# Two factors' first columns as one stretch of a weight tile, its rows loaded in two halves by two queues

## The chip, the cores and the metric

The kernel runs on one core of a Trainium2 chip. The metric is the device time of one execution in microseconds (us); less is better. A kernel's time is the median of its runs.

## What is computed

For eight sequences of 128 tokens with 512 features, `x` goes through a linear layer with a low-rank adapter chosen for each sequence, then through a second linear layer with a routed low-rank part (the best two of 16 experts), and the input is added at the end. Cut to what matters:

```python
base_out = jnp.einsum('bti,oi->bto', x, W) + b               # L0_cond: W is 512 x 512
A, Bm = lora_As[adapter_mapping], lora_Bs[adapter_mapping]    # one adapter of 32 for a sequence
y = base_out + jnp.einsum('btr,bro->bto', jnp.einsum('bti,bir->btr', x, A), Bm) * 2.0

base_out = jnp.einsum('bsi,oi->bso', y, base_w) + base_b      # L0_ffn
res_hidden = jnp.einsum('bsi,ri->bsr', y, A)                  # R = 64
probs = jax.nn.softmax(jnp.einsum('bsi,ei->bse', y, router_w), axis=-1)
topw, topi = jax.lax.top_k(probs, 2)                          # of 16 experts, then normalised
delta = jnp.einsum('bse,bsr,eor->bso', combine, res_hidden, B)
out = x + base_out + delta * 0.5
```

## The kernel before

**The fold.** The two linear layers follow each other with nothing between them, so the kernel first multiplies their weights into one: W is one factor and the second layer's three matrices side by side (64 + 16 + 512 = 592 columns) are the other. On the way in, both stand beside each other in `w_cat`, in four chunks `k` of 128 rows: columns 0 to 511 are W, columns 512 to 1103 the second factor. The tile `w_raw` has the same layout in SBUF: 128 partitions, chunk `k`, 1104 columns. The product of chunk `k` is summed over `k` in four pairs of PSUM banks, `pairs[0]` to `pairs[3]`; pair `m` takes the 128 columns `m*128` to `m*128+127` of W as its stationary side.

**Split products.** To keep float32 accuracy every factor is split in a high and a low part (`w_hi`, `w_lo`), and every product is three matmuls: high by high, high by low, low by high. The high part is a cast (on ScalarE for W's columns, on VectorE for the second factor's), the low part a subtraction on VectorE.

**The start.** Chunk 0 is loaded in four pieces. ScalarE issues W's left half (`W_LEFT`, columns 0 to 255) and then its right half (`W_RIGHT`). SyncE issues the second factor's left half (`W2_LEFT`, 296 columns) and then its right half (`W2_RIGHT`). Each piece covers all 128 partitions and has a semaphore of its own. As pieces land, ScalarE casts W's left half in two steps of 128 columns and then the right half in one; VectorE casts `W2_LEFT`, subtracts for `W2_LEFT` and `W_LEFT`, casts `W2_RIGHT`, subtracts for `W2_RIGHT` and `W_RIGHT`. TensorE runs 13 matmuls on a tile of zeros (`WARM_UP`), and then the fold of chunk 0 in quarters: first the pairs of the first half of W's columns (m = 0, 1) against `W2_LEFT`, then against `W2_RIGHT`, then the other two pairs likewise. Each quarter has three groups of two matmuls, and each group waits for its operands: `wh_left`/`wh_done` count ScalarE's casts, `wh_first` VectorE's, `wl_first` and `wl_done` VectorE's subtractions. Chunks 1 to 3 follow whole, the one behind the other, on every engine.

**After the fold** the eight sequences go through as a pipeline: products of x with the folded weights, routing, expert products. Every engine's order is written out by hand; semaphores alone order the engines among each other.

All matmuls are issued by the helper `mm` at L820, so that the profile has one line for all of them.

Of the kernel before, what the change touches and what calls it, by code (L numbers as in the profile page):

```python
# [15 lines left out]
ACT = mybir.ActivationFunctionType  # L16
AX_X = mybir.AxisListType.X

P = 128
NT = 8  # L20
D = 512
KC = D // P
# [31 lines left out]
FOLDS = (1, 0, 2, 3)  # L54

W_LEFT, W_RIGHT = slice(0, D // 2), slice(D // 2, D)
W2_LEFT, W2_RIGHT = slice(D, D + W2H), slice(D + W2H, D + W2N)
WARM_UP = 13

ACT_TABLES = 2  # L60
# [2 lines left out]
def adaln_ffn_kernel(nc, x_t, x_n, w_cat, tables, slots, b1, b2, experts, out):  # L63
    with ExitStack() as ctx:
# [6 lines left out]
        def sem(name):  # L71
            return ctx.enter_context(nc.semaphore(name))
# [5 lines left out]
        w_raw = w_raw_all[:, :].rearrange("p (k n) -> p k n", k=KC)  # L78
# [10 lines left out]
        w_hi = w_hi_all[:, :].rearrange("p (k n) -> p k n", k=KC)  # L89
# [85 lines left out]


        in_w = [None] + [sem(f"in_w{k}") for k in range(1, KC)]
        in_w_side = [sem("in_w_left"), sem("in_w_right")]
        in_w2_side = [sem("in_w2_left"), sem("in_w2_right")]
        in_w_next = sem("in_w_next")  # L180
        in_slots = sem("in_slots")
        in_lora = sem("in_lora")
# [9 lines left out]
        stored = sem("stored")  # L192

        wh_first = sem("wh_first")
        wh_left = sem("wh_left")
        wh_next = sem("wh_next")
        wh_done = sem("wh_done")
        wl_first = sem("wl_first")
        wl_done = sem("wl_done")
# [59 lines left out]
        def _(sp):  # L259
# [1 line left out]
                sp.dma_start(w_raw[:, k, :], w_cat[k]).then_inc(in_w[k], 16)  # L261


            for n, cols in enumerate((W2_LEFT, W2_RIGHT)):
                sp.dma_start(w_raw[:, 0, cols], w_cat[0, :, cols]).then_inc(in_w2_side[n], 16)

            sp.dma_start(w_raw[:, 1, D // 2:], w_cat[1, :, D // 2:]).then_inc(in_w[1], 16)
            sp.dma_start(w_raw[:, 1, W_LEFT], w_cat[1, :, W_LEFT]).then_inc(in_w_next, 16)
# [86 lines left out]
            for half in range(2):  # L355
                cols = slice(half * D // 2, (half + 1) * D // 2)
# [56 lines left out]

        @block.scalar
        def _(act):
            for n, cols in enumerate((W_LEFT, W_RIGHT)):
                act.dma_start(w_raw[:, 0, cols], w_cat[0, :, cols]).then_inc(in_w_side[n], 16)
            act.wait_ge(in_w_side[0], 16)
            for cols in (slice(0, P), slice(P, 2 * P)):
                nc.scalar.activation(w_hi[:, 0, cols], w_raw[:, 0, cols], ACT.Copy).then_inc(wh_left, 1)  # L420
            act.wait_ge(in_w_side[1], 16)
            nc.scalar.activation(w_hi[:, 0, W_RIGHT], w_raw[:, 0, W_RIGHT], ACT.Copy).then_inc(wh_done, 1)
            act.wait_ge(in_slots, 16)
            for t in range(NT - ACT_TABLES, NT):
                slot = act.value_load(slot_row[0:1, t:t + 1], min_val=0, max_val=SLOTS - 1)
# [160 lines left out]
        def _(dve):  # L586
# [10 lines left out]
            nc.vector.memset(low_row[F_BIAS:F_BIAS + 1, :], 0.0).then_inc(first_set, 1)  # L597

            def first_block_hi(n, cols):
                dve.wait_ge(in_w2_side[n], 16)  # L600
                nc.vector.tensor_copy(w_hi[:, 0, cols], w_raw[:, 0, cols]).then_inc(wh_first, 1)

            def first_block_lo(cols, done):
                nc.vector.tensor_tensor(w_lo[:, 0, cols], w_raw[:, 0, cols], w_hi[:, 0, cols].bitcast(F32),
                                        ALU.subtract).then_inc(done, 1)

            first_block_hi(0, W2_LEFT)
            dve.wait_ge(wh_first, 1)
            first_block_lo(W2_LEFT, wl_first)
            dve.wait_ge(wh_left, 2)  # L610
            first_block_lo(W_LEFT, wl_done)
            first_block_hi(1, W2_RIGHT)
            dve.wait_ge(wh_first, 2)
            first_block_lo(W2_RIGHT, wl_first)
            dve.wait_ge(wh_done, 1)
            first_block_lo(W_RIGHT, wl_done)
            for k in range(1, KC):
                dve.wait_ge(in_w[k], 16)
                nc.vector.tensor_copy(w_hi[:, k, D:], w_raw[:, k, D:]).then_inc(wh_first, 1)
# [190 lines left out]
            for half in range(2):  # L810
                cols = slice(half * D // 2, (half + 1) * D // 2)
# [6 lines left out]
        def _(pe):  # L818
            def mm(out_ap, lhs, rhs, first, last):
                return nc.tensor.matmul(out_ap, lhs, rhs, start=first, stop=last)  # L820
# [5 lines left out]

            for _ in range(WARM_UP):
                mm(ps_warm, idle[:, 0:P], idle, True, True)
# [6 lines left out]
            def fold_quarter(m, lhs, rhs, out_cols, cols, first):  # L835
                mm(pairs[m][:, out_cols], lhs[:, 0, m * P:(m + 1) * P], rhs[:, 0, cols], first, False)

            sides = ((slice(BANK - W2H, BANK), W2_LEFT), (slice(BANK, BANK + W2H), W2_RIGHT))
            for half, rows_done in enumerate((wh_left, wh_done)):
                ms = range(half * KC // 2, (half + 1) * KC // 2)  # L840
                for side, (out_cols, cols) in enumerate(sides):
                    pe.wait_ge(wh_first, side + 1)
                    for m in ms:
                        pe.wait_ge(rows_done, 1 if half else m + 1)
                        fold_quarter(m, w_hi, w_hi, out_cols, cols, True)
                    pe.wait_ge(wl_first, side + 1)
                    for m in ms:
                        fold_quarter(m, w_hi, w_lo, out_cols, cols, False)
                    pe.wait_ge(wl_done, half + 1)
                    for m in ms:  # L850
                        fold_quarter(m, w_lo, w_hi, out_cols, cols, False)
# [240 lines left out]
```

## Time and profile before

| | us |
|---|---|
| median of three runs | 101.38 |
| lowest, highest | 101.21, 102.25 |
| the profiled execution, its whole time | 101.33 |
| the span of its instructions | 99.5 |
| TensorE busy in the span | 95.6 |
| VectorE, ScalarE, GpSimd busy | 66.6, 41.5, 22.2 |

The whole time of the profiled execution is 1.83 us more than its span: what lies around the instructions. The trace is of that one execution. Its times are in us from the start of the span; engines are PE (TensorE matmuls), PEld (its weight loads), DVE (VectorE), ACT (ScalarE), POOL (GpSimd) and SP (SyncE); a q behind a name is the engine's sequencer, which issues the DMAs.

### The profile page before, as it was taken

The page shows a single profiled execution, that of the slowest core. Times are in us where ns is not written, and L with a number is a line of the kernel's source. Part 1 is how long each engine was busy: PE and PEld are TensorE (multiplying, and loading weights), DVE is VectorE, ACT ScalarE, POOL GpSimd, SP SyncE. Part 2 cuts the span into 40 slices and gives each one's busy share as a digit, 9 for nine tenths or more (in the row PEclk, how much of TensorE's full clock was granted, in tenths as well). Part 3 has the DMA queues.
Part 4 walks back from the last instruction along what each step waited for, and adds up shares of the span by engine and source line. Part 5 has one row for each costly group of instructions (what it writes and reads, how often), then busy time and mean ns, then how long its engine had stood idle before and what let it go on. Part 6 is the DMA issues. An engine that isn't in the chain of part 4 may idle for free.

```text
span 99.5 us, 1810 instructions
## 1 busy us (share of the span) xinstructions
PE 95.6 (96%) x572; PEld 87.0 (87%) x572; DVE 66.6 (67%) x184; ACT 41.5 (42%) x101; POOL 22.2 (22%) x34
## 2 busy tenths in 40 slices
PE   6799999999999999999999999999999999999990
PEld 6699999999999999998898799888787877878980
DVE  5669996997485885899977567257949275572101
ACT  3514636968787546756522610451334022040000
POOL 4100004224999965108123000000000000000000
PEclk9999999999999999999999999999999999999999
DMA  1999659999558675891780836516228074020211
GB/s 42 331 326 410 207 123 361 267 361 352 150 91 205 203 239 151 232 231 37 221 253 25 214 119 163 153 43 184 106 76 255 26 194 122 0 105 0 105 59 53
DMA packets 8379, 16.91 MB, mean 170 GB/s; under 512 B 1507, under 2 KB 4067, under 8 KB 8370
## 3 DMA queue, kind: packets, MB, share of 16 engines
q1 hardware_dynamic: 7762, 16.41, 55.1%
q10 hardware_dynamic: 576, 0.39, 1.2%
q8 instruction: 5, 0.08, 0.3%
q14 instruction: 4, 0.03, 0.1%
q0 software_dynamic: 32, 0.00, 0.0%
HBM read 13.28 MB, written 2.16 MB: 155 GB/s over the span
## 4 chain that ended last, share of the span: by engine, by line
PE 93%; DMA 3%; DVE 0%; ACT 0%; issue 0%
PE pair L820 90%; DMA w_raw_all<-w_cat 3%; PE pair L965 1%; PE pair L967 1%; PE pair L985 1%; DVE xn L814 0%; ACT w_hi_all L420 0%; PE pair L955 0%; PE pair L944 0%; PE pair L942 0%; PE pair L934 0%
## 5 line engine op out<-in xcount | busy, mean ns | idle before, releaser
L820 PE MATMUL pair<-e_hi,w_hi_all 128*128 128x512 f32 (+1 forms) x72 | 27.1, 376 | 0.0
L820 PE MATMUL pair<-e_hi,w_lo_all 128*128 128x512 f32 (+1 forms) x72 | 26.7, 370 | 0.0
L820 PE MATMUL pair<-e_lo,w_hi_all 128*128 128x512 f32 (+1 forms) x72 | 26.7, 370 | 0.0
L533 ACT ACTIVATE w_hi_all<-exp_raw_all 128x512 fp32r<-128x512 f32 x16 | 9.7, 630 | 15.3 <-DVE exp_raw_all L755 15.3
L820 PEld LDWEIGHTS pair<-e_hi,w_lo_all 128*128 128x128 f32 x72 | 13.6, 188 | 2.5
L820 PEld LDWEIGHTS pair<-e_hi,w_hi_all 128*128 128x128 f32 x72 | 13.6, 188 | 2.5
L820 PEld LDWEIGHTS pair<-e_lo,w_hi_all 128*128 128x128 f32 x72 | 13.6, 189 | 2.0
L762 DVE TENSOR_TENSOR w_lo_all<-exp_raw_all,w_hi_all 128x512 fp32r<-128x512 f32 x16 | 10.4, 689 | 4.5 <-ACT w_hi_all L533 4.0
L755 DVE TENSOR_TENSOR exp_raw_all<-w_raw_all 128x512 f32<-128x512 f32 x16 | 11.2, 741 | 0.1
L769 DVE TENSOR_TENSOR xn<-pair,xn 128x512 f32<-128x512 f32 x7 | 4.8, 690 | 8.9 <-PE pair L820 8.9
L820 PE MATMUL pair<-p_hi,x_hi 128*128 128x304 f32 x32 | 10.0, 311 | 0.0
L820 PE MATMUL pair<-p_hi,w_hi_all 128*128 128x304 f32 x32 | 9.9, 308 | 0.0
L820 PE MATMUL pair<-p_lo,x_hi 128*128 128x304 f32 x32 | 9.7, 303 | 0.0
L820 PE MATMUL pair<-p_lo,w_hi_all 128*128 128x304 f32 x32 | 9.7, 302 | 0.0
L820 PE MATMUL pair<-p_hi,w_lo_all 128*128 128x304 f32 x32 | 9.7, 302 | 0.0
L820 PE MATMUL pair<-p_hi,x_lo 128*128 128x304 f32 x32 | 9.7, 302 | 0.0
L376 POOL TENSOR_TENSOR w_lo_all<-xt_raw,w_hi_all 128x512 fp32r<-128x512 f32 x4 | 5.2, 1293 | 13.7 <-ACT w_hi_all L438 10.6
L394 POOL TENSOR_TENSOR e_lo<-exp_raw_all,e_hi 128x1024 fp32r<-128x1024 f32 x3 | 7.2, 2399 | 0.0
L820 PE MATMUL pair<-w_hi_all 128*128 128x296 f32 x32 | 6.1, 301 | 0.5 <-ACT w_hi_all L420 0.5
L820 PEld LDWEIGHTS pair<-p_hi,w_hi_all 128*128 128x128 f32 x32 | 6.0, 188 | 0.3
L820 PEld LDWEIGHTS pair<-p_lo,w_hi_all 128*128 128x128 f32 x32 | 6.0, 189 | 0.2
L820 PE MATMUL pair<-w_lo_all,w_hi_all 128*128 128x296 f32 x32 | 6.1, 302 | 0.0
(107 smaller groups left out, 162.2 us busy)
## 6 DMA issues: line engine op xcount, KB each, us to landing
w_raw_all<-spill SPq DMA_DIRECT2D x16, 256.0 KB, 4.2
xt_raw<-x_t SPq DMA_DIRECT2D x4, 512.0 KB, 6.3
exp_raw_all<-experts SPq DMA_DIRECT2D x4, 512.0 KB, 8.7
xn<-x_n SPq DMA_DIRECT2D x4, 512.0 KB, 5.8
out<-xn SPq DMA_DIRECT2D x7, 256.0 KB, 2.8
w_raw_all<-w_cat SPq DMA_DIRECT2D x2, 552.0 KB, 6.4
c_stack<-c_hi SPq DMA_DIRECT2D x7, 74.0 KB, 3.9
c_stack<-c_lo SPq DMA_DIRECT2D x7, 74.0 KB, 4.2
```

What stands on the lines that cost most here:

```text
L376: pool.tensor_tensor(x_los[t % XB], xt_raw[:, t, :].rearrange("p (k n) -> p k n", k=KC), x_his[t % XB].bitcast(F32), ALU.subtract).then_in ...
L394: pool.tensor_tensor(e_lo[:, js, :], exp_raw[:, js, :], e_hi[:, js, :].bitcast(F32), ALU.subtract).then_inc(el_pool_done, 1)
L533: nc.scalar.activation(gt_hi[:, t % 2, js, :], g[:, js, :], ACT.Copy).then_inc(gh_done, 1)
L755: nc.vector.tensor_tensor(g[:, js, :], weight_rows[:, b, js, :], hidden[:, b, :].unsqueeze(1).to_broadcast([P, GH, P]), ALU.mult).then_inc ...
L762: nc.vector.tensor_tensor(gt_lo[:, t % 2, js, :], g[:, js, :], gt_hi[:, t % 2, js, :].bitcast(F32), ALU.subtract).then_inc(gl_done, 1)
L769: nc.vector.tensor_tensor(xn[:, t, :], ps_d[t % 2], xn[:, t, :], ALU.add).then_inc(out_done, 1)
L820: return nc.tensor.matmul(out_ap, lhs, rhs, start=first, stop=last)
L965: nc.tensor.matmul(ps_z[par][:, z_small[par]:BANK], ht[:, par, :], c_stack[0:HT, t, 0:border], start=False, stop=True, skip_group_check=True)
L967: nc.tensor.matmul(ps_z[par][:, BANK:BANK + W2N - border], ht[:, par, :], c_stack[0:HT, t, border:], start=False, stop=True, skip_group_ch ...
L985: nc.tensor.transpose(ps_rt[0:cols, :], routed[:, t % 2, 0:cols], ident[:, :]).then_inc(pe_rt, 1)
```

## The change

Chunk 0 is cut into pieces in another way. W's right half and the second factor's left half are neighbours in `w_cat` and in `w_raw`; together they are one stretch of 552 columns, `LEAD` (columns 256 to 807). This stretch is now the first piece. SyncE loads its rows 0 to 63, ScalarE its rows 64 to 127, and both transfers count on one semaphore, `in_lead`. Behind its half SyncE loads `W2_RIGHT` as before, and ScalarE loads W's left half, which is now `W_REST`. The fold of chunk 0 begins with the pairs 2 and 3 (W's right half) and goes on to 0 and 1. Both ScalarE's first cast and VectorE's first cast wait for `in_lead` to reach 32, that is for both halves of the rows. The names `wh_left` and `in_w_side`, `in_w2_side` go.

```diff
+W_LEAD, W_REST = W_RIGHT, W_LEFT
 W2_LEFT, W2_RIGHT = slice(D, D + W2H), slice(D + W2H, D + W2N)
+LEAD = slice(W_LEAD.start, W2_LEFT.stop)
...
-            for n, cols in enumerate((W2_LEFT, W2_RIGHT)):
-                sp.dma_start(w_raw[:, 0, cols], w_cat[0, :, cols]).then_inc(in_w2_side[n], 16)
+            sp.dma_start(w_raw[0:P // 2, 0, LEAD], w_cat[0, 0:P // 2, LEAD]).then_inc(in_lead, 16)
+            sp.dma_start(w_raw[:, 0, W2_RIGHT], w_cat[0, :, W2_RIGHT]).then_inc(in_w2_right, 16)
...
-            for n, cols in enumerate((W_LEFT, W_RIGHT)):
-                act.dma_start(w_raw[:, 0, cols], w_cat[0, :, cols]).then_inc(in_w_side[n], 16)
-            act.wait_ge(in_w_side[0], 16)
-            for cols in (slice(0, P), slice(P, 2 * P)):
-                nc.scalar.activation(w_hi[:, 0, cols], w_raw[:, 0, cols], ACT.Copy).then_inc(wh_left, 1)
-            act.wait_ge(in_w_side[1], 16)
-            nc.scalar.activation(w_hi[:, 0, W_RIGHT], w_raw[:, 0, W_RIGHT], ACT.Copy).then_inc(wh_done, 1)
+
+            act.dma_start(w_raw[P // 2:, 0, LEAD], w_cat[0, P // 2:, LEAD]).then_inc(in_lead, 16)
+            act.dma_start(w_raw[:, 0, W_REST], w_cat[0, :, W_REST]).then_inc(in_rest, 16)
+            act.wait_ge(in_lead, 32)
+            for cols in (slice(2 * P, 3 * P), slice(3 * P, 4 * P)):
+                nc.scalar.activation(w_hi[:, 0, cols], w_raw[:, 0, cols], ACT.Copy).then_inc(wh_lead, 1)
+            act.wait_ge(in_rest, 16)
+            nc.scalar.activation(w_hi[:, 0, W_REST], w_raw[:, 0, W_REST], ACT.Copy).then_inc(wh_done, 1)
...
             def first_block_hi(n, cols):
-                dve.wait_ge(in_w2_side[n], 16)
+                if n == 0:
+                    dve.wait_ge(in_lead, 32)
+                else:
+                    dve.wait_ge(in_w2_right, 16)
...
-            for half, rows_done in enumerate((wh_left, wh_done)):
-                ms = range(half * KC // 2, (half + 1) * KC // 2)
+            for half, rows_done in enumerate((wh_lead, wh_done)):
+
+                ms = range((1 - half) * KC // 2, (2 - half) * KC // 2)
```

ScalarE's queue at the start of the program, before: two transfers of all 128 rows, then the table load and the casts of W's columns, each half behind its own semaphore.

```order
L417 DMA w_raw_all<-w_cat 128x256 x2
L420 ACT_TABLE_LOAD
L420 ACTIVATE w_hi_all<-w_raw_all 128x128 [waits in_w_left]
L420 ACTIVATE w_hi_all<-w_raw_all 128x128
L422 ACTIVATE w_hi_all<-w_raw_all 128x256 [waits in_w_right]
```

ScalarE's queue at the same place, now:

```order
L421 DMA w_raw_all<-w_cat 64x552
L422 DMA w_raw_all<-w_cat 128x256
L425 ACT_TABLE_LOAD
L425 ACTIVATE w_hi_all<-w_raw_all 128x128 [waits in_lead]
L425 ACTIVATE w_hi_all<-w_raw_all 128x128
L427 ACTIVATE w_hi_all<-w_raw_all 128x256 [waits in_rest]
```

The casts stand where they stood; the first transfer has half the rows and a little over twice the columns, and the first cast waits for the semaphore on which SyncE's half counts too.

VectorE's queue for chunk 0, before:

```order
L601 CAST w_hi_all<-w_raw_all 128x296 [waits in_w2_left]
L604 TENSOR_TENSOR w_lo_all<-w_raw_all,w_hi_all 128x296 [waits wh_first]
L604 TENSOR_TENSOR w_lo_all<-w_raw_all,w_hi_all 128x256 [waits wh_left]
L601 CAST w_hi_all<-w_raw_all 128x296 [waits in_w2_right]
L604 TENSOR_TENSOR w_lo_all<-w_raw_all,w_hi_all 128x296 [waits wh_first]
L604 TENSOR_TENSOR w_lo_all<-w_raw_all,w_hi_all 128x256 [waits wh_done]
```

VectorE's queue for chunk 0, now:

```order
L609 CAST w_hi_all<-w_raw_all 128x296 [waits in_lead]
L612 TENSOR_TENSOR w_lo_all<-w_raw_all,w_hi_all 128x296 [waits wh_first]
L612 TENSOR_TENSOR w_lo_all<-w_raw_all,w_hi_all 128x256 [waits wh_lead]
L609 CAST w_hi_all<-w_raw_all 128x296 [waits in_w2_right]
L612 TENSOR_TENSOR w_lo_all<-w_raw_all,w_hi_all 128x296 [waits wh_first]
L612 TENSOR_TENSOR w_lo_all<-w_raw_all,w_hi_all 128x256 [waits wh_done]
```

The six steps keep their order and their sizes; the first of them no longer waits for SyncE's piece alone.

## Rows read from the trace of the kernel before

**Rows 1.** The page, part 1: busy us, share of the span, instructions of each engine.

```profile
PE 95.6 (96%) x572; PEld 87.0 (87%) x572; DVE 66.6 (67%) x184; ACT 41.5 (42%) x101; POOL 22.2 (22%) x34
```

**Rows 2.** The chain that ended last, in order of time: start us, us, what.

```profile
0.74 3.15 DMA w_raw_all<-w_cat
...
3.92 0.32 ACT w_hi_all L420
...
4.37 20.75 PE pair L820 x148
...
96.98 0.42 DVE xn L814
```

**Rows 3.** SyncE's two transfers of chunk 0 (L265): issue ns, starts, landing.

```profile
L265 SPq DMA_DIRECT2D w_raw_all<-w_cat x2: 401/406/412, 0.7 to 1.2; - x2
...
DMA to landing us min/median/max: 3.0/3.1/3.2
```

**Rows 4.** ScalarE's two transfers of chunk 0 (L417): the same columns.

```profile
L417 ACTq DMA_DIRECT2D w_raw_all<-w_cat x2: 413/436/458, 0.7 to 1.2; - x2
...
DMA to landing us min/median/max: 3.2/3.2/3.3
```

**Rows 5.** VectorE's timeline from 3.6 us: start, us, instruction [idle before <-releaser].

```profile
3.73 0.32 DVE L601 CAST w_hi_all<-w_raw_all 128x296 fp32r<-128x296 f32 x1 [0.58 <-DMA w_raw_all<-w_cat]
4.08 0.80 DVE L604 TENSOR_TENSOR w_lo_all<-w_raw_all,w_hi_all 128x296 fp32r<-128x296 f32 x2
4.80 0.31 DVE L601 CAST w_hi_all<-w_raw_all 128x296 fp32r<-128x296 f32 x1
5.14 0.81 DVE L604 TENSOR_TENSOR w_lo_all<-w_raw_all,w_hi_all 128x296 fp32r<-128x296 f32 x2
6.64 0.47 DVE L619 CAST w_hi_all<-w_raw_all 128x592 fp32r<-128x592 f32 x1 [0.69 <-DMA w_raw_all<-w_cat]
```

**Rows 6.** ScalarE's timeline from 3.6 us, the same columns.

```profile
3.92 0.51 ACT L420 ACTIVATE w_hi_all<-w_raw_all 128x128 fp32r<-128x128 f32 x2 [0.96 <-DMA w_raw_all<-w_cat]
4.55 0.42 ACT L422 ACTIVATE w_hi_all<-w_raw_all 128x256 fp32r<-128x256 f32 x1
```

**Rows 7.** TensorE's timeline to 8 us, matmuls (PE) and weight loads (PEld).

```profile
0.78 3.04 PE L820 MATMUL pair<-const-float32-0.0 128*128 128x256 f32 x13 [0.78 <-PEq L1085]
...
4.37 0.51 PE L820 MATMUL pair<-w_hi_all 128*128 128x296 f32 x2 [0.55 <-ACT w_hi_all L420]
...
4.72 0.43 PE L820 MATMUL pair<-w_lo_all,w_hi_all 128*128 128x296 f32 x2
...
5.32 0.43 PE L820 MATMUL pair<-w_hi_all 128*128 128x296 f32 x2
...
5.66 0.30 PEld L820 LDWEIGHTS pair<-w_lo_all,w_hi_all 128*128 128x128 f32 x2 [0.16 <-DVE w_lo_all L604]
5.67 0.54 PE L820 MATMUL pair<-w_lo_all,w_hi_all 128*128 128x296 f32 x2
...
6.32 0.44 PE L820 MATMUL pair<-w_hi_all 128*128 128x296 f32 x2
...
7.95 1.26 PE L820 MATMUL pair<-w_hi_all 128*128 128x296 f32 x8
```

**Rows 8.** Five stretches: us, busy time of each engine, granted clock, DMA share, GB/s.

```profile
2.50:3.40 0.90, 0.90 (x6) 0.90 (x6) 0.40 (x5) 0.46 (x1) 0.35 (x3) 1.00 1.08 377
22.20:23.50 1.30, 1.30 (x12) 1.30 (x11) 1.23 (x2) 1.14 (x3) 0.00 (x0) 1.00 1.04 410
60.60:63.30 2.70, 2.70 (x19) 2.48 (x18) 1.97 (x4) 0.00 (x0) 0.00 (x0) 1.00 0.97 245
80.00:82.70 2.70, 2.70 (x13) 2.17 (x12) 2.50 (x4) 1.24 (x2) 0.00 (x0) 1.00 0.94 227
96.98:99.40 2.42, 0.00 (x0) 0.00 (x0) 0.42 (x1) 0.00 (x0) 0.00 (x0) 0.96 0.16 54
```

**Rows 9.** DMA issues from 59.3 to 63.3 us: times, KB each, us to landing.

```profile
w_raw_all<-spill SPq DMA_DIRECT2D x2, 256.0 KB, 3.9
```

More of the change, by code:

```diff
@@ L177, in adaln_ffn_kernel @@
         in_w = [None] + [sem(f"in_w{k}") for k in range(1, KC)]
-        in_w_side = [sem("in_w_left"), sem("in_w_right")]
-        in_w2_side = [sem("in_w2_left"), sem("in_w2_right")]
+        in_lead = sem("in_lead")
+        in_rest = sem("in_rest")
+        in_w2_right = sem("in_w2_right")
         in_w_next = sem("in_w_next")
@@ L194, in adaln_ffn_kernel @@
         wh_first = sem("wh_first")
-        wh_left = sem("wh_left")
+        wh_lead = sem("wh_lead")
         wh_next = sem("wh_next")
@@ L609, in _ @@
             first_block_lo(W2_LEFT, wl_first)
-            dve.wait_ge(wh_left, 2)
-            first_block_lo(W_LEFT, wl_done)
+            dve.wait_ge(wh_lead, 2)
+            first_block_lo(W_LEAD, wl_done)
             first_block_hi(1, W2_RIGHT)
@@ L615, in _ @@
             dve.wait_ge(wh_done, 1)
-            first_block_lo(W_RIGHT, wl_done)
+            first_block_lo(W_REST, wl_done)
             for k in range(1, KC):
@@ L838, in _ @@
             sides = ((slice(BANK - W2H, BANK), W2_LEFT), (slice(BANK, BANK + W2H), W2_RIGHT))
-            for half, rows_done in enumerate((wh_left, wh_done)):
-                ms = range(half * KC // 2, (half + 1) * KC // 2)
+            for half, rows_done in enumerate((wh_lead, wh_done)):
+                ms = range((1 - half) * KC // 2, (2 - half) * KC // 2)
                 for side, (out_cols, cols) in enumerate(sides):
                     pe.wait_ge(wh_first, side + 1)
-                    for m in ms:
-                        pe.wait_ge(rows_done, 1 if half else m + 1)
+                    for n, m in enumerate(ms):
+                        pe.wait_ge(rows_done, 1 if half else n + 1)
                         fold_quarter(m, w_hi, w_hi, out_cols, cols, True)
```

## The prediction

> **What bounds the kernel now.** I read the page first: TensorE is busy for 95.6 of 99.5 us [rows 1], no other engine for more than 67 percent. The chain of waits followed back from the end says the same: from 4.37 us on it is all TensorE, and ahead of that stand one transfer, one cast of ScalarE and nothing else [rows 2]. So a change to the loads of chunk 0 can act only through the moment from which TensorE runs without a break. The reader should now look for that moment, and it is not 4.37. The fold's first pair of matmuls starts at 4.37, released by ScalarE's cast. Undisturbed, a pair takes about 0.27 us from start to start: from the pair at 6.32 to the eight matmuls at 7.95 lie six pairs in 1.63 us. At the beginning pairs start at 4.37, 4.72, 5.32 and 5.67, and at 5.66 the weight load is idle for 0.16 us until VectorE's subtraction (L604) [rows 7]. TensorE is fed there by VectorE, whose row of work has no hole: it begins at 3.73 with the cast, goes on at 4.08, 4.80, 5.14 and is through at 5.95 [rows 5]. Behind 5.67 TensorE waits for nobody, and its operands are there early: chunk 1 is cast by VectorE at 6.64 to 7.11 [rows 5] and wanted at 7.95 [rows 7].
>
> The moment that decides is therefore the **start of VectorE's first cast**, 3.73 us, set by the landing of SyncE's first piece: issued at 0.75, landed 3.0 us later [rows 3]. ScalarE's first piece lands 0.2 us later, at 3.2 us behind an issue at 0.74 [rows 4], and ScalarE starts at 3.92 [rows 6]. That W's left half comes later costs the first pair of matmuls something, but not the end of the chunk, as long as VectorE is the one that is late at 5.67.
>
> **The change, part by part.**
>
> *The wait of VectorE (the term that counts).* VectorE's first cast used to wait for SyncE's 148 KB alone. It now waits for both halves of the lead piece, 138 KB on each queue. Queued behind it on VectorE are the five other steps of chunk 0; TensorE waits for each of them. The two first pieces hold 276 KB before and after, so the last byte of them should land when the last byte lands now, which is ScalarE's 3.9 us. If so, VectorE starts at 3.92 instead of 3.73: **+0.19 us**. All six steps move by that much, and with them the group of matmuls that waits for the subtraction at 5.67: it starts at 5.86. Nothing behind it can give that back, since TensorE is then busy to the end.
>
> *Size of the packets, a gain.* The rows of the lead piece are 2208 bytes long, where they were 1024 and 1184. The rate of the two first pieces in flight together is 377 GB/s (2.50 to 3.40 us); the best stretch of long rows over all partitions has 410 [rows 8]. 276 KB are 282.6 thousand bytes, 0.75 us at the one and 0.69 us at the other: at most 0.06 us earlier.
>
> *Half the partitions, a loss.* No transfer of the kernel before loads 64 rows from each of two queues. The nearest rows are the loads of routing weights from DRAM, each 256 KB for 64 partitions [rows 9]: in the stretches in which they fill the engines (share 0.97 and 0.94) these move 245 and 227 GB/s, not 377 to 410 [rows 8]. If the two halves ran at the slower of these, 282.6 thousand bytes would take 1.25 us, 0.50 us more than 0.75. But there one queue works through one half of the partitions and then the other, and each source row is read for 64 partitions. Here the halves are issued within 0.01 us of each other from two queues and run at the same time over all 128 partitions, as the two pieces do now. The nearest row for that is the present start, 377 GB/s. I take the loss of the halves and the gain of the longer rows as equal, together 0, and keep both ends: the landing moves by −0.06 to +0.50 us, VectorE's start by +0.13 to +0.69 us.
>
> The Trainium skill has a rule against this change, on its page "DMA: Bandwidth & Descriptors", section "Rules for kernel authors": of two transfers to disjoint halves of the partitions it says "Don't bother — they serialize", because both halves spread over the same 16 DMA engines. What the row shows is less than a queue for one: SyncE's and ScalarE's first pieces land 0.2 us apart though 128 KB alone need 0.35 us at 377 GB/s, so two pieces from two queues share the engines, they do not follow each other. Read to the letter, the rule would put the second half 0.37 us (138 KB at 377 GB/s) behind a first one that lands at 3.7, at 4.07, and the sum would be +0.34 instead of +0.19 us.
>
> *ScalarE and TensorE's first pair.* ScalarE starts its casts at 3.92 as before (3.86 at the best). VectorE's cast needs 0.32 us and ScalarE's first step about as long [rows 2, 5], so the operands of the first matmul are there at 4.24 and it starts at 4.37, as now: **0**. The next group needs the subtraction, which ends at 4.74 instead of 4.55 and so pushes the pair from 4.72 to about 4.87. These small gaps are the same 0.19 us, seen earlier; they are not added.
>
> *The other pieces.* `W2_RIGHT` lands 3.2 us behind an issue at 1.2, at 4.36 [rows 3]; VectorE now wants it at 4.80 + 0.19. ScalarE's second piece lands 3.3 us behind 1.2 and its cast runs from 4.55 to 4.97 [rows 4, 6]; TensorE wants it at 6.32. Both have 0.4 us or more to spare: **0**. The order of the pairs (2, 3 before 0, 1) changes no count and no size: **0**. The number of transfers is the same, and an issue of 0.4 us stays one of 0.4 us: **0**, and the queues behind are where they were. Chunk 1 lets VectorE idle for 0.69 us at 6.64 [rows 5], which takes up any delay of its own; TensorE's delay is not taken up.
>
> **The sum.** 101.33 (this execution) + 0.19 = 101.52 us. This execution lies 0.05 us under the median of the runs, so against the median it is 101.38 + 0.19 = **101.57 us**. That is 0.2 percent more. About 1 percent, 1.0 us, is what a measurement of this kernel can tell from no change.
>
> **Rivals.**
>
> *The halves are slow (loss up to 0.50 us).* For it speaks the rate of the loads for 64 partitions. The Trainium skill ("DMA: Bandwidth & Descriptors", section "The descriptor swizzle") says that in a transfer over 128 partitions each DMA engine writes one port of its own, and engines 0 to 7 write partitions 0 to 63; a half that spreads over all 16 would share ports. The trace shows no ports. Against it speaks that both halves run together. It gives +0.34 to +0.69 us, 101.7 to 102.1.
>
> *The piece lands earlier than SyncE's does now.* Longer rows might be worth more than the row of 410 GB/s shows, or SyncE's and ScalarE's halves might be closer to the present first landing at 3.7. Then ScalarE starts up to 0.2 us earlier, VectorE no later than now, and the first block ends where it ends today or up to 0.13 us earlier: 101.25 to 101.4. Against it: the whole 276 KB must be there, and 0.2 us of 377 GB/s are 75 KB that nobody takes off the engines.
>
> *VectorE's start isn't what decides.* If TensorE's group at 5.67 has slack that the trace hides, the start of the first matmul counts, and that doesn't move: 101.38, no effect. Against it is the hole of 0.16 us at 5.66.
>
> *Slower by over 1 percent: the clock.* The 13 warm-up matmuls of 256 columns take 3.04 us, 0.21 us from start to start, which is 1.2 GHz; the fold's 296 columns take 0.136 us, which is near 2.4 GHz [rows 7] (the clock row gives 1.00 for both, so the cadence has to tell). Between them TensorE is idle for 0.55 us. If late halves stretch this hole to 1 us and the clock then falls, as much work as the warm-up fills, 3.04 us at the low level, costs half of it too much: +1.5 us on top of the +0.69, 103.6. The point is whether the longer hole lets the clock fall. Against it: behind the last matmul, TensorE has nothing to do for 2.42 us and the mean granted clock of that stretch is still 0.96 [rows 8]; so most of 2 us of idleness leave it at the upper level. And with an unchanged first matmul the hole doesn't grow at all.
>
> **How the numbers follow.** Chances: 0.60 for the forecast (VectorE +0.13 to +0.33 us, 101.5 to 101.7); 0.20 for slow halves; 0.10 for an earlier landing; 0.06 for no effect; 0.02 for the clock; 0.02 for what I don't see. The range takes in the forecast, no effect, slow halves and the earlier landing, and some 0.1 us at the lower end for the spread of the runs (the lowest is 0.17 under the median): 101.15 to 102.1. Only the clock's case lies over 1 percent, and with a stray median I give it 0.04; no case reaches 1 percent faster, since the whole wait for the first piece would have to shrink by a third, and a stray median gets 0.02; within 1 percent 0.94.
>
> **What the profile of the changed kernel would show.** Right: VectorE's first cast and ScalarE's first cast start within 0.05 us of each other, near 3.9; the first fold matmul near 4.37; a wait for VectorE's subtraction of about 0.2 us or more ahead of the fifth group; that group near 5.86; TensorE without a break behind it; and the span 0.2 us longer. Slow halves: both casts at 4.1 to 4.4. Earlier landing: both at 3.75 or before. No effect: the casts late, but the eight matmuls of chunk 1 still at 7.95 and not at 8.14. The clock: fold matmuls 0.25 us apart behind the hole. I would be wrong above all if half-height transfers from two queues get in each other's way in a manner that no row of this trace shows.

## The result, and the profile after

The changed kernel is slower: **103.46 us** (102.46 to 104.62, six runs) against 101.35 (101.21 to 102.25). The ratio is **1.0135, with a 95% interval of 1.0085 to 1.0185**. The forecast was 101.57 with a range up to 102.1; the time lies outside it. The ratio and its interval, here and in all experiments, leave out runs over 1.5 percent above the fastest of the same kernel (here 104.62, which is the profiled one, and 104.52), so they are not the quotient of the medians.

The profiled execution of the changed kernel took 104.62 us, the longest of the six, and its span is 102.8. Not all of the 3.3 us that the span has over that of before is the change's. The chain of the kernel after, in order of time (start us, us, what):

```profile
0.76 3.48 DMA w_raw_all<-w_cat
...
4.26 0.32 DVE w_hi_all L609
...
4.71 22.31 PE pair L828 x148
27.03 0.11 PE pair L943
...
98.88 0.42 DVE xn L822
```

The last addition starts at 98.88 where it started at 96.98 [rows 2]: 1.90 us later. The other 1.4 us lie behind it, where only the last stores are left and nothing was changed. (An experiment below, the one with the joined wait, has the same: its last addition is at 96.95 and its span 100.9.) So the reader should use a mark inside the program. I take TensorE's **first transposition**, L943 here at 27.03, the first line after the 148 matmuls. The same piece in the chain of the kernel before:

```profile
25.13 0.11 PE pair L934
```

It too is 1.90 us later. The whole difference ahead of the last stores arises before the mark, and from there both kernels run alike up to the last addition. (1.90 us is the distance of two single executions; the one of the kernel before took 101.33 us, less than most of its runs beside the experiments.)

TensorE's timeline of the kernel after, to 10 us:

```profile
4.71 0.83 PE L828 MATMUL pair<-w_hi_all 128*128 128x296 f32 x2 [0.82 <-DVE w_hi_all L609]
5.34 0.69 PE L828 MATMUL pair<-w_lo_all,w_hi_all 128*128 128x296 f32 x2
5.84 0.69 PE L828 MATMUL pair<-w_hi_all,w_lo_all 128*128 128x296 f32 x2
...
8.30 0.63 PE L828 MATMUL pair<-w_lo_all,w_hi_all 128*128 128x296 f32 x2
8.77 0.44 PE L828 MATMUL pair<-w_hi_all,w_lo_all 128*128 128x296 f32 x2
9.04 0.44 PE L828 MATMUL pair<-w_hi_all 128*128 128x296 f32 x2
```

The first matmul is 0.34 us late, where the prediction had it unchanged at 4.37. And then pairs of matmuls (two matmuls that the trace shows as one row) start 0.49 us apart, 0.247 us for one of 296 columns: that is 1.2 GHz, the lower level of TensorE's clock. Only from 8.77 on are they 0.27 us apart, the cadence that the kernel before has in its fold [rows 7]. Up to its ninth pair the kernel before needs 2.50 us (4.37 to 6.87), this one 4.06: 1.56 us more. 0.34 + 1.56 is the 1.90 us. The 1.56 us are less than the clock alone costs: eight pairs at 0.272 us would be 2.18 us, so the low clock costs 1.88 us, and the 0.32 us that TensorE lost between its first pairs before [rows 7] no longer show. The matmuls have no idle stretch between them; the loss doesn't show in any list of waits, and the granted clock of the stretch reads 1.00. What tells is the distance from start to start. (The low clock isn't special to this long execution: experiments 6 and 10 have it in profiled executions of 103.60 and 103.17 us.)

ScalarE's timeline of the kernel after:

```profile
0.76 0.57 ACTq L421 DMA_DIRECT2D w_raw_all<-w_cat  x1
1.37 0.84 ACTq L422 DMA_DIRECT2D w_raw_all<-w_cat  x1
2.24 1.28 ACT L425 ACT_TABLE_LOAD   x1 [2.24 <-issue]
4.26 0.51 ACT L425 ACTIVATE w_hi_all<-w_raw_all 128x128 fp32r<-128x128 f32 x2 [0.74 <-DMA w_raw_all<-w_cat]
6.61 0.42 ACT L427 ACTIVATE w_hi_all<-w_raw_all 128x256 fp32r<-128x256 f32 x1 [1.84 <-DMA w_raw_all<-w_cat]
7.49 1.42 ACTq L432 DMA_DIRECT2D lora_raw<-tables  x2
8.96 0.72 ACT L435 ACTIVATE w_hi_all<-w_raw_all 128x256 fp32r<-128x256 f32 x2 [1.93 <-issue]
```

Two things here answer to [rows 4] and [rows 6]. The issues of the transfers take 0.57 and 0.84 us, where both took 0.41 to 0.46. And `W_REST` is cast at 6.61, not at 4.55: its transfer, issued at 1.37, needs 5.2 us to land, where the piece in its place needed 3.3. Behind it ScalarE's slot loads and adapter transfers are late, and with them its casts for chunk 1.

SyncE's half and ScalarE's half of the lead (L268 and L421), first the one, then the other:

```profile
L268 SPq DMA_DIRECT2D w_raw_all<-w_cat x1: 571/571/571, 0.7 to 0.7; - x1
...
DMA to landing us min/median/max: 2.9/2.9/2.9
```

```profile
L421 ACTq DMA_DIRECT2D w_raw_all<-w_cat x1: 570/570/570, 0.8 to 0.8; - x1
...
DMA to landing us min/median/max: 3.5/3.5/3.5
```

The halves are issued together and land 0.6 us apart, at 3.7 and 4.2.

### The profile page after: what moved, and what is told of

The parts are those of the page before. It is cut to its first block, busy times and chain, and to the rows that moved or that the text cites. A ratio compares the mean times of both kernels' runs of the same rounds, so it can differ in the third digit from the quotient of the medians.

```text
span 102.8 us, 1810 instructions
## 1 busy us (share of the span) xinstructions
PE 97.2 (95%) x572; PEld 88.8 (86%) x572; DVE 66.3 (64%) x184; ACT 41.4 (40%) x101; POOL 21.8 (21%) x34
## 4 chain that ended last, share of the span: by engine, by line
PE 92%; DMA 3%; DVE 1%; issue 0%
PE pair L828 88%; DMA w_raw_all<-w_cat 3%; PE pair L974 1%; PE pair L976 1%; PE pair L994 1%; DVE xn L822 0%; DVE w_hi_all L609 0%; PE pair L964 0%; PE pair L953 0%; PE pair L951 0%; PE pair L943 0%
## 5 line engine op out<-in xcount | busy, mean ns | idle before, releaser
L828 PE MATMUL pair<-w_hi_all 128*128 128x296 f32 x32 | 6.9, 331 | 0.8 <-DVE w_hi_all L609 0.8
L828 PE MATMUL pair<-w_lo_all,w_hi_all 128*128 128x296 f32 x32 | 6.7, 325 | 0.0
L828 PE MATMUL pair<-w_hi_all,w_lo_all 128*128 128x296 f32 x32 | 6.5, 317 | 0.0
L828 PEld LDWEIGHTS pair<-w_hi_all 128*128 128x128 f32 x32 | 5.6, 214 | 1.1 <-DVE w_hi_all L609 1.1
```

## The experiments

There are three suspects: the low clock, the late `W_REST`, and the transfers of 64 rows behind both. Theories A to D are those of each experiment's own expectation; a letter doesn't mean the same in all of them. Times are compared as ratios, since the kernel before measured 101.9 to 102.0 beside these runs. The hole is TensorE's idle time between its last warm-up matmul and the first one of the fold. The mark is the first transposition of one profiled execution each: 25.13 before, 27.03 after.

**1. More warm-up in the changed kernel.** TensorE's hole ahead of the fold is filled.

```diff
-WARM_UP = 13
+WARM_UP = 18
```

> The changed kernel with 18 warm-up matmuls instead of 13, which fills TensorE's idle stretch ahead of the fold (3.89 to 4.71 us in the profile after). Theory A (most of the 2 us come from the fold running at the low level of TensorE's clock, since the hole of 0.82 us keeps the clock from rising): the fold's matmuls are back at 0.136 us from start to start early on, and the time falls from 103.5 to about 102.0 (what is left is the later start and the late W_REST). Theory B (the loads alone cost it: lead piece at 4.24, W_REST at 6.59): no better than 103.3, or worse by the added warm-up.

103.29 us, ratio 1.0106 (1.0024 to 1.0187), mark at 27.11. Five of the six runs lie at 103.3 to 103.5 and one at 101.84. Theory A, which had 102.0, falls in this form. TensorE's timeline of this kernel:

```profile
4.69 0.51 PE L828 MATMUL pair<-w_hi_all 128*128 128x296 f32 x2 [0.20 <-DVE w_hi_all L609]
...
6.54 0.43 PE L828 MATMUL pair<-w_hi_all,w_lo_all 128*128 128x296 f32 x2
7.46 0.51 PE L828 MATMUL pair<-w_hi_all 128*128 128x296 f32 x2 [0.49 <-ACT w_hi_all L427]
7.80 0.44 PE L828 MATMUL pair<-w_lo_all,w_hi_all 128*128 128x296 f32 x2
...
9.86 0.92 PE L828 MATMUL pair<-w_hi_all 128*128 128x296 f32 x5 [0.53 <-ACT w_hi_all L435]
```

The clock is up from the first fold matmul, as theory A wanted, and nothing is won: TensorE now waits twice, at 7.46 for the cast of `W_REST` and at 9.86 for ScalarE's cast of chunk 1. In the changed kernel's own profile these waits were hidden, since TensorE at half speed came to both places when the data was there. From the first matmul of the fold to the first of chunk 1 the kernel before needs 3.58 us (4.37 to 7.95 [rows 7]), this one 5.17 (4.69 to 9.86) and the changed kernel 5.15 (4.71 to 9.86). So two costs of about 1.6 us cover for each other.

**2. The same in the kernel before.** `WARM_UP = 18` there.

> The kernel before with 18 warm-up matmuls instead of 13. At the low level the warm-up then ends at about 4.9 us, 0.5 us behind the present start of the fold. Theory A: the hole of 0.55 us goes, the spread of the kernel before (101.2 to 102.25) shrinks, the median lies between 101.2 and 101.8. Theory B: the fold starts up to 0.5 us later, 101.6 to 101.9, and the spread stays.

101.65 us, ratio 0.9999 (0.9957 to 1.0041), mark at 25.45. The longer warm-up is neither a gain nor a loss within what this can tell. In the one execution the fold starts at 4.60, 0.23 us later, and the mark is 0.32 us later; the spread stays (101.1 to 102.6), as theory B had it.

**3. Only the joined wait.** The kernel before, with VectorE's first cast behind both first pieces.

```diff
             def first_block_hi(n, cols):
+                if n == 0:
+                    dve.wait_ge(in_w_side[0], 16)
                 dve.wait_ge(in_w2_side[n], 16)
```

> The kernel before, with one more wait: VectorE's first cast also waits for ScalarE's first piece, as in the change; all transfers as before. By the prediction's sum +0.19 us (101.55). If joining the two waits is what matters beyond that, 102 or more; if the transfers in halves matter, it stays at 101.4 to 101.6.

102.28 us, ratio 1.0019 (0.9974 to 1.0063), mark at 25.10. In this execution ScalarE's piece landed early enough that both casts began at 3.71; the forecast's 0.19 us can't be told from zero here, and by the interval the joined wait alone costs 0.6 us at most.

**4. Only the order of the work.** The changed kernel with whole-height pieces and a semaphore for each.

```diff
-            sp.dma_start(w_raw[0:P // 2, 0, LEAD], w_cat[0, 0:P // 2, LEAD]).then_inc(in_lead, 16)
+            sp.dma_start(w_raw[:, 0, W2_LEFT], w_cat[0, :, W2_LEFT]).then_inc(in_w2_left, 16)
...
-            act.dma_start(w_raw[P // 2:, 0, LEAD], w_cat[0, P // 2:, LEAD]).then_inc(in_lead, 16)
+            act.dma_start(w_raw[:, 0, W_LEAD], w_cat[0, :, W_LEAD]).then_inc(in_lead, 16)
...
```

ScalarE's first cast waits for `in_lead` to reach 16, VectorE's for `in_w2_left`.

> The changed kernel's order of work (pairs 2 and 3 first, W's right half loaded first) with the transfers of the kernel before: each piece over all 128 partitions with a semaphore of its own. Theory A and B alike, both of which blame the transfers in halves: 101.3 to 101.6, as before. If the order of the pairs costs something: 102 or more.

102.06 us, ratio 1.0002 (0.9960 to 1.0044), mark at 25.13. The order of the pairs costs nothing that can be told, as forecast. With the joined wait out too, the lead piece in halves is what is left, as a long stretch or as half the height; the next two experiments separate these.

**5. The lead stretch in one piece.** SyncE loads all 128 rows of it, ScalarE only `W_REST`.

```diff
-            sp.dma_start(w_raw[0:P // 2, 0, LEAD], w_cat[0, 0:P // 2, LEAD]).then_inc(in_lead, 16)
+            sp.dma_start(w_raw[:, 0, LEAD], w_cat[0, :, LEAD]).then_inc(in_lead, 16)
...
-            act.dma_start(w_raw[P // 2:, 0, LEAD], w_cat[0, P // 2:, LEAD]).then_inc(in_lead, 16)
...
```

Both waits for `in_lead` go from 32 to 16.

> The changed kernel with the lead stretch in one transfer of all 128 rows, from SyncE; ScalarE issues W_REST alone. Theory A (transfers of 64 rows are slow to be issued and to begin: 0.57 us where 128 rows took 0.41, and the two halves run one behind the other): the lead's issue is back at about 0.41 us, it lands at 3.9 or before, W_REST lands by 4.6, the fold's last-but-early marker (the first transposition of TensorE) stands near 25.1 to 25.3 instead of 27.0 us, the time is as before. Theory B (the long rows of 2208 bytes are what is slow): the issue stays at 0.57 us or more, the lead lands at 4.2 or later.

102.09 us, ratio 1.0037 (1.0011 to 1.0064), mark at 25.21. The lead transfer of this kernel:

```profile
L268 SPq DMA_DIRECT2D w_raw_all<-w_cat x1: 402/402/402, 0.7 to 0.7; - x1
...
DMA to landing us min/median/max: 3.0/3.0/3.0
```

The same 552 columns, twice the rows and the bytes, and it is issued in 0.40 us and lands at 3.8, before the second half does in the changed kernel. The width is innocent. The loss isn't quite gone: the interval lies 0.1 to 0.6 percent above the kernel before.

**6. Halves at the narrow widths.** The kernel before, its two first pieces each as two halves of 64 rows.

```diff
+            sp.dma_start(w_raw[0:P // 2, 0, W2_LEFT], w_cat[0, 0:P // 2, W2_LEFT]).then_inc(in_w2_side[0], 16)
+            sp.dma_start(w_raw[0:P // 2, 0, W_LEFT], w_cat[0, 0:P // 2, W_LEFT]).then_inc(in_w_side[0], 16)
...
+            act.dma_start(w_raw[P // 2:, 0, W2_LEFT], w_cat[0, P // 2:, W2_LEFT]).then_inc(in_w2_side[0], 16)
+            act.dma_start(w_raw[P // 2:, 0, W_LEFT], w_cat[0, P // 2:, W_LEFT]).then_inc(in_w_side[0], 16)
...
```

`W2_RIGHT` and `W_RIGHT` follow whole; the first casts wait for both halves of their piece.

> The kernel before with its two first pieces each cut in halves of 64 rows over the two queues, at their narrow widths (296 and 256 columns); two transfers more in all. Theory A (half height is what costs): each half takes as long to issue as the wide halves did, about 0.57 us, so the first pieces land past 4.4 and W_RIGHT past 6.5, and the first transposition stands at 27 us or later. Theory B (width costs): issues of 0.41 us and less, first transposition by 25.6.

103.58 us, ratio 1.0158 (1.0107 to 1.0208), mark at 27.28. Its transfers by ScalarE, two of 64 rows and then one of 128:

```profile
0.76 0.57 ACTq L417 DMA_DIRECT2D w_raw_all<-w_cat  x1
1.35 0.86 ACTq L418 DMA_DIRECT2D w_raw_all<-w_cat  x1
2.25 0.60 ACTq L419 DMA_DIRECT2D w_raw_all<-w_cat  x1
2.89 1.28 ACT L422 ACT_TABLE_LOAD   x1 [2.89 <-issue]
```

0.57 us again at 296 columns: it is the height that makes the issue long. The transfer of 128 rows right behind the halves is slow too: `W_RIGHT` 0.60 us, `W2_RIGHT` 0.59, where both took 0.40 to 0.46 before. The halves of `W_LEFT`, second on both queues, are complete at 4.6 (forecast above 4.4), `W_RIGHT` at 5.4 (forecast above 6.5, a miss), the hole is 1.16 us and the matmuls are 0.247 us apart until 8.65. But the halves of `W2_LEFT`, first on both queues, aren't late at all (a miss of the same forecast). VectorE casts them 0.38 us earlier than the whole piece before:

```profile
3.35 0.31 DVE L603 CAST w_hi_all<-w_raw_all 128x296 fp32r<-128x296 f32 x1 [0.21 <-DMA w_raw_all<-w_cat]
```

So half the height doesn't by itself make a transfer land late. What is late here is the piece whose halves are issued second, at 1.35 us instead of 0.74.

**7. `W_REST` on time.** The changed kernel, SyncE issues `W_REST` behind `W2_RIGHT`.

```diff
+            sp.dma_start(w_raw[:, 0, W_REST], w_cat[0, :, W_REST]).then_inc(in_rest, 16)
...
-            act.dma_start(w_raw[:, 0, W_REST], w_cat[0, :, W_REST]).then_inc(in_rest, 16)
```

> The changed kernel with W_REST issued by SyncE, behind W2_RIGHT and ahead of chunk 1, instead of by ScalarE. Theory A (the late landing of W_REST at 6.6 to 6.9, in between chunk 1's long rows, is most of the loss, and ScalarE's queue behind it): W_REST lands at about 5.0, the first transposition stands at 25.4 to 25.8 instead of 27.0, the time falls by 1.2 us or more against the changed kernel. Theory B (the later lead piece or the clock is most of it): the marker stays above 26.5.

103.63 us, ratio 1.0119 (1.0062 to 1.0175), mark at 27.28: no gain that can be told, theory A misses again. `W_REST` is cast at 5.69, and TensorE never waits after its first matmul, but its hole is 0.91 us and the cadence is the slow one up to 8.89:

```profile
4.80 0.83 PE L828 MATMUL pair<-w_hi_all 128*128 128x296 f32 x2 [0.91 <-DVE w_hi_all L609]
...
8.39 0.69 PE L828 MATMUL pair<-w_lo_all,w_hi_all 128*128 128x296 f32 x2
8.89 0.57 PE L828 MATMUL pair<-w_hi_all,w_lo_all 128*128 128x296 f32 x2
```

**8. A late second piece alone.** The kernel before; ScalarE issues `W_RIGHT` behind its first casts.

```diff
-            for n, cols in enumerate((W_LEFT, W_RIGHT)):
-                act.dma_start(w_raw[:, 0, cols], w_cat[0, :, cols]).then_inc(in_w_side[n], 16)
+            act.dma_start(w_raw[:, 0, W_LEFT], w_cat[0, :, W_LEFT]).then_inc(in_w_side[0], 16)
...
+            act.dma_start(w_raw[:, 0, W_RIGHT], w_cat[0, :, W_RIGHT]).then_inc(in_w_side[1], 16)
             act.wait_ge(in_w_side[1], 16)
```

> The kernel before with one thing made late: ScalarE issues W_RIGHT behind its first two casts, at about 4.4 us, instead of at 1.2. Everything else lands as before. Theory A: W_RIGHT lands near 7 us, TensorE has run out of work at 6.3 and the first transposition moves from 25.1 to 26.5 or later, like the changed kernel, though the first pieces are on time. Theory B: the marker stays under 25.8.

108.47 us, ratio 1.0623 (1.0569 to 1.0678). The direction is theory A's, the size is not: the chain of this kernel

```profile
3.82 7.08 DMA w_raw_all<-w_cat
...
10.92 0.42 ACT w_hi_all L422
...
11.48 19.59 PE pair L820 x125
```

has a transfer of 128 KB that takes 7.08 us, since it is issued behind all of SyncE's loads of chunks 1 to 3 and x. TensorE is idle for 4.48 us, and behind that idle time its clock is low (0.247 us from start to start) until 16.4; here the granted clock shows it, 0.50 from 10 to 16.4 us. That the long transfers ahead on the other queue are what makes this one slow is an argument from its place; for the sum of the change it is too strong a dose.

**9. Both followers away.** Experiments 1 and 7 in one: the halves stay, `W_REST` comes from SyncE, 18 warm-up matmuls.

> The changed kernel, halves and all, with both suspected followers taken away together: W_REST issued by SyncE ahead of chunk 1, and 18 warm-up matmuls. Theory C (the halves cost about 0.4 us at the start of the fold; the rest of the loss is one of two things that cover for each other: the fold's first 4 us at the low level of the clock, or, with the clock up, TensorE waiting for W_REST; undoing one alone shows the other): the first transposition stands at 25.5 to 25.9 us instead of 27.0, the time is 0.3 to 0.9 us over the kernel before. Theory D (a third thing): it stays above 26.5.

102.31 us, ratio **1.0042 (1.0014 to 1.0069)**, mark at 26.32. The time falls to where theory C has it; the mark doesn't, it misses 25.9 by 0.4 us, since in this execution `W_REST` is cast at 6.16 (5.69 in experiment 7) and TensorE still waits for ScalarE's cast of chunk 1:

```profile
4.60 0.51 PE L828 MATMUL pair<-w_hi_all 128*128 128x296 f32 x2
...
9.07 1.32 PE L828 MATMUL pair<-w_hi_all 128*128 128x296 f32 x8 [0.48 <-ACT w_hi_all L435]
```

Of 12 runs all lie between 101.8 and 102.5.

**10. A shorter warm-up alone.** The kernel before with `WARM_UP = 9`: no transfer and no wait is touched. The hole grows, and TensorE has also done four matmuls less when it begins.

> The kernel before with 9 warm-up matmuls instead of 13: the hole ahead of the fold is 1.4 us instead of 0.55, no transfer changes. Theory C: the clock doesn't rise before about 8 us, the fold's matmuls start 0.247 us apart until then, the first transposition moves from 25.1 to 26.7 or later and the time rises by 1 to 2 us. If the hole is without effect on the clock: 25.1 and 101.4 to 101.9.

103.36 us, ratio **1.0155 (1.0100 to 1.0210)**, mark at 26.96. The loads are on time, the first fold matmul is even 0.15 us earlier than in the profile of before, and still the mark is 1.83 us later, nearly as in the changed kernel:

```profile
4.22 0.83 PE L820 MATMUL pair<-w_hi_all 128*128 128x296 f32 x2 [1.18 <-ACT w_hi_all L420]
4.85 0.69 PE L820 MATMUL pair<-w_lo_all,w_hi_all 128*128 128x296 f32 x2
...
8.79 0.60 PE L820 MATMUL pair<-w_hi_all 128*128 128x296 f32 x2
9.24 0.44 PE L820 MATMUL pair<-w_lo_all,w_hi_all 128*128 128x296 f32 x2
```

How much of this is the longer hole and how much the four matmuls that are missing ahead of it, this run doesn't separate. Experiments 6 and 7 and the changed kernel have all 13 matmuls.

**11. Both halves from one queue.** SyncE issues the two halves, ScalarE only `W_REST`.

```diff
+            sp.dma_start(w_raw[P // 2:, 0, LEAD], w_cat[0, P // 2:, LEAD]).then_inc(in_lead, 16)
...
-            act.dma_start(w_raw[P // 2:, 0, LEAD], w_cat[0, P // 2:, LEAD]).then_inc(in_lead, 16)
```

> The changed kernel with both halves of the lead issued by SyncE, one behind the other; ScalarE issues W_REST alone. If a transfer of 64 rows is slow by itself, each half takes 0.57 us to issue and the second lands at 4.2 or later. If it is the two queues issuing such halves at once, the issues fall to about 0.4 us, though the second half still starts one issue later and lands at 4.0 to 4.3. W_REST, issued at 0.75, lands by 4 in both cases.

103.41 us, ratio 1.0109 (1.0064 to 1.0153), mark at 25.96. SyncE's queue in this kernel, two halves and `W2_RIGHT`, then a piece of chunk 1:

```profile
0.74 0.57 SPq L268 DMA_DIRECT2D w_raw_all<-w_cat  x1
1.37 0.57 SPq L269 DMA_DIRECT2D w_raw_all<-w_cat  x1
1.99 0.58 SPq L270 DMA_DIRECT2D w_raw_all<-w_cat  x1
2.62 0.43 SPq L272 DMA_DIRECT2D w_raw_all<-w_cat  x1
```

A transfer of 64 rows is slow to issue by itself, also when both halves come from one queue; so is the one of 128 rows behind them (0.58 us), and only the next is back at 0.43. The second half lands at 4.55. `W_REST`, now first on ScalarE's queue, is issued in 0.40 us and lands at 3.0. The twelve times are in two groups, five from 102.2 to 102.5 and seven from 103.4 to 104.0. The profile fell in the first: in spite of a hole of 1.13 us the fold runs at the fast cadence from its start at 5.03. So whether a hole of this length costs the clock isn't the same in every execution.

**12. A version that might beat both.** The kernel before with `WARM_UP = 16`.

> The kernel before with 16 warm-up matmuls: at the low level they end at about 4.5 us, where the fold begins, so that the hole goes and the fold is delayed by no more than 0.1 us (18 matmuls delayed it by 0.2 to 0.4). If the hole of 0.55 us now and then costs the kernel before its clock too, this should be the best version: the slower runs get rarer and the median falls by 0.2 to 0.5 us against the kernel before. If it never does, the two are the same.

101.70 us, ratio 0.9996 (0.9959 to 1.0033), mark at 25.52. No better. No version here beats the kernel before. Its profile has something to teach all the same:

```profile
4.33 0.71 PE L820 MATMUL pair<-w_hi_all 128*128 128x296 f32 x2
...
5.82 0.51 PE L820 MATMUL pair<-w_hi_all 128*128 128x296 f32 x2
6.17 0.44 PE L820 MATMUL pair<-w_lo_all,w_hi_all 128*128 128x296 f32 x2
```

There is no hole, and the fold still starts at the low clock: its pairs are 0.50 us apart up to 5.82.

| kernel | clock low in the fold, in the profile | TensorE waits for ScalarE | mark, us | ratio |
|---|---|---|---|---|
| changed | until 8.8 us | no | 27.03 | 1.0135 |
| 1: hole filled | no | 0.49 + 0.53 us | 27.11 | 1.0106 |
| 7: `W_REST` from SyncE | until 8.9 us | no | 27.28 | 1.0119 |
| 9: both | no | 0.48 us | 26.32 | 1.0042 |
| 10: 9 warm-up matmuls, loads as before | until 9.2 us | no | 26.96 | 1.0155 |
| 5: lead in one piece | only the first pair | no | 25.21 | 1.0037 |
| 12: 16 warm-up matmuls, loads as before | until 5.8 us | no | 25.52 | 0.9996 |

Over all profiled executions, one of each kernel: with a hole of 0.82 us or more (the changed kernel, 6, 7, 10, 11) the fold is at the low clock until 8.3 us or later in four of five; with 0.55 us or less (the kernel before and the other eight) it is at the upper one by 6.3 us at the latest in all nine.

## Why the prediction was wrong

**What bounds the kernel: right.** Nothing behind the fold moved; the change acted through the start of it alone, and no later stage gave anything back or took more.

**The joined wait, +0.19 us: the wrong size, from a wrong landing.** VectorE's first cast starts at 4.26, 0.53 us later than at 3.73 [rows 5]. That lies inside the bounds of +0.13 to +0.69, nearer the upper one. ScalarE's first cast went from 3.92 to 4.26 by the same landing, and the first matmul, which was given 0, from 4.37 to 4.71: +0.34. The step that failed is "Here the halves are issued within 0.01 us of each other from two queues and run at the same time over all 128 partitions", and the row taken for it, 377 GB/s. They don't run like the two pieces before: they land 0.6 us apart, at 3.7 and 4.2. The row of the loads for 64 partitions was the better guide (its bound for the landing was 4.4), and so was the Trainium skill's "they serialize" ("DMA: Bandwidth & Descriptors", "Rules for kernel authors"), which gave 4.07 for the second half; this trace has 4.24. Why it is 4.24 stays open: the same bytes in one transfer are there at 3.8 (experiment 5), and two narrow halves issued first land early (experiment 6).

**"An issue of 0.4 us stays one of 0.4 us: 0": wrong.** It stands at 0.57 us for 64 rows whatever the width, and at 0.56 to 0.84 us for the transfer of 128 rows behind them (the kernel after, experiments 6 and 11). The trace of before had it, in the loads for 64 partitions that the prediction took its rate from; their issues take 0.55 us in the median:

```profile
L335 SPq DMA_DIRECT2D w_raw_all<-spill x16: 451/547/599, 34.1 to 79.4; - x16
```

It is a part of what makes the later transfers late.

**"The other pieces ... 0": wrong, and dear.** `W_REST` was given 0.4 us or more to spare. It lands 2.1 us later. With the clock up that stops TensorE twice (experiment 1: 0.49 and 0.53 us). The step had asked when the piece was wanted, and had taken it for granted that it would land when it did. But it is now issued at 1.37 to 2.21 instead of 1.2 to 1.6 and shares the DMA engines with chunk 1's rows of 3392 bytes; experiment 8 has the same in excess (7.08 us). That the long rows are the cause and not the later issue alone is an argument from these two landings; it wasn't taken apart.

**"Its operands are there early": half read.** The prediction looked at VectorE's cast of chunk 1 and not at ScalarE's, which stands behind the first casts and ScalarE's own transfers in its queue. In the kernel before it is this one:

```profile
7.13 0.73 ACT L430 ACTIVATE w_hi_all<-w_raw_all 128x256 fp32r<-128x256 f32 x2 [2.16 <-DMA w_raw_all<-w_cat]
```

In experiments 1, 2 and 9, where TensorE waits for this cast, it goes on 0.55 to 0.56 us after the cast began. By that the operands are there at 7.69 before, and chunk 1 is wanted at 7.95: an estimate of 0.26 us to spare. In the kernel after the cast begins at 8.96. So chunk 1 couldn't have started before about 9.52 (an estimate too) at either clock, and started at 9.86: at the upper clock this execution would have won back no more than 0.34 us.

**The clock, given 0.02: the rival that came true in this profile, by another mechanism.** It was named with its place, and what it predicted of the profile (matmuls 0.25 us apart behind the hole) is what the profile shows. Two steps led away from it. One is "with an unchanged first matmul the hole doesn't grow at all": the first matmul came at 4.71, and the hole went from 0.55 to 0.82 us. The other is the argument from the end of the program, where 2.42 us of idleness left the clock up [rows 8]. That row is about a clock that has been up for 90 us. At the start it has yet to rise. In the profile of before it comes up at the end of the warm-up: the 13 matmuls are through at 3.82 [rows 7], 0.07 us sooner than the same 13 in the profile of after, and the fold begins at the fast cadence. In that of after the clock isn't up yet when the hole begins, and then it comes as late as 8.8 us. So the hole didn't make the clock fall. That it kept it from rising fits four of the five profiles with a hole of 0.82 us or more, but the hole isn't all that decides: in experiment 11 the clock was up behind a hole of 1.13 us, and in experiment 12 it was low up to 5.8 us with no hole. Experiment 10 shows what a late rise costs when no load is touched: 1.0155. The size, 1.5 us forecast and 1.56 measured in the profile, was right by luck: 1.5 was half of 3.04 us at the low level, while the fold was there for 4.06 us, and 0.32 us of waits came off.

**The sum again, as the profile of after has it:** 0.34 us for the first matmul, 1.56 us for eight pairs at the low level, 0 for waits, in all 1.90 us at the mark. Over the six runs the loss is 2.1 us in the medians, and 1.4 us by the ratio. How often an execution of the changed kernel pays with the clock, and how often with the waits, stays open: one profile shows one execution. That both exist and cost nearly the same is shown by experiments 1, 7 and 9; undoing one brings nothing that can be told, undoing both takes the ratio from 1.0135 to 1.0042. What is left, about 0.4 us, is the size that the rival of slow halves had (+0.34 to +0.69 us).

## What to carry to other kernels

A transfer cut in halves of 64 rows isn't two times half a transfer: count its issue and its landing from a row of the same height, and look at what is queued behind it on both queues. When two costs are undone one at a time and neither gives anything back, undo both before dropping the theory; a slow engine hides the waits that it would have had. At a program's start the distance between matmuls belongs among the first things to read: in these traces the low clock there shows neither as idle time nor in the granted clock, which reads 1.00.

## What the runs showed that was not expected

- Issue of a transfer from DRAM to SBUF: 0.57 us for 64 rows of 296 or 552 columns, 0.40 us for 128 rows of 552. Right behind one of 64 rows, one of 128 rows takes 0.56 to 0.60 us instead of 0.40 to 0.46, and the second one on ScalarE's queue 0.84 us (128 rows, the kernel after) or 0.86 (64 rows, experiment 6).
- Nine warm-up matmuls instead of 13, and with them a hole of 1.18 us ahead of the first product, with the loads on time, cost 1.6 percent (1.0 to 2.1). A hole of 1.13 us behind 13 left the clock alone in one profiled execution of another kernel, and 16 matmuls without a hole left it low up to 5.8 us in a third: when the clock rises isn't told by the hole alone.
- Behind the last addition the span of one execution may be 1.4 us longer than another's with the same work (2.1 us from 97.4 to the end of the span before, 3.5 from 97.4 with the joined wait). From the mark to the end of the whole time it is 76.2 us in the kernel before and in experiments 1, 2, 5, 9, 10 and 12, up to 76.6 in 6, 7 and 11, and 77.1 to 77.6 in 3, 4 and the changed kernel. So the whole time of a single execution says little of a change at the start; a mark inside the program does.
